# Three edits to a 12-stage decoder kernel: half-width value projections, array halves in turn, a bias on another engine, tables loaded last

## The reference

```python
# "table" attention: layer 0 self (rope) and cross (ctx), layer 2 router block (rank), layer 3 cross (mask)
q, k, v = xn @ Wq + bq, kv @ Wk + bk, kv @ Wv + bv          # kv = xn or the context rows
p = softmax(q @ k.T * scale + table)                        # table: a bias per head, 64 x 64
x = x + (p @ v) @ Wo + bo
# linear attention: layer 1 self
fq, fk = elu(q) + 1, elu(k) + 1
s = (fk @ fq.T) * (key index <= query index)
y = xn + ((s.T @ v) / (s.T @ 1 + 1e-6)) @ Wo + bo
# dense block that ends layer 2 self-attention
x = x + y + gelu(norm(y) @ W1 + b1) @ W2 + b2
```

## Time and profile before

| | |
|---|---|
| median of 3 runs | 7626.08 us (7619.54 to 7646.74) |
| profiled execution, its own time | 7625.12 us |
| its span, first to last instruction | 7623.3 us |
| PE busy over the span | 6668.1 us (87%) |
| DVE, ACT, POOL busy | 5380.2, 4152.7, 2881.5 us |
| mean granted TensorE clock | 0.950 |

### The profile page before, as it was taken

One profiled execution on the slowest core, in us unless ns is written; L12 is line 12 of the kernel. 1 busy time (PEld: TensorE's weight loads), 2 busy tenths in 40 slices (PEclk: granted clock), 3 DMA queues, 4 the chain that ended last, 5 costly groups with the idle time before them and its releaser, 6 DMA issues. The chain is left out here.

```text
span 7623.3 us, 190380 instructions
## 1 busy us (share of the span) xinstructions
PE 6668.1 (87%) x75040; PEld 4091.5 (54%) x75040; DVE 5380.2 (71%) x8861; ACT 4152.7 (54%) x6107; POOL 2881.5 (38%) x1663
## 2 busy tenths in 40 slices
PE   7989994887687989979988968989889999989898
PEld 5766683443442333333333345667566676667676
DVE  7877465575546999969999944668567777768444
ACT  3555333565435777767777754546444444446433
POOL 3311163332214888868787800146012121111000
PEclk9999996999888999989999989999999999999999
DMA  1000001000001222212222100000000000000000
GB/s 27 0 17 15 2 0 17 3 3 2 8 2 52 75 72 73 76 56 78 72 70 72 67 3 18 12 4 0 3 29 2 2 2 2 2 13 14 13 0 22
DMA packets 117004, 191.53 MB, mean 25 GB/s; under 512 B 39542, under 2 KB 75420, under 8 KB 116060
## 3 DMA queue, kind: packets, MB, share of 16 engines
q1 hardware_dynamic: 116572, 185.25, 7.7%
HBM read 174.99 MB, written 8.09 MB: 24 GB/s over the span
## 5 line engine op out<-in xcount | busy, mean ns | idle before, releaser
L2461 POOL TENSOR_TENSOR m_dBx<-m_dtx,m_Bs 128x1024 f32<-128x1024 f32 x518 | 1211.2, 2355 | 211.6 <-DVE m_hs L2798 169.3
L2798 DVE TENSOR_TENSOR_SCAN m_hs<-m_ps_dA,m_dBx 128x512 f32<-128x512 f32 x1036 | 1207.4, 1207 | 87.0 <-POOL m_dBx L2461 77.0
L2577 PE MATMUL m_ps_y<-m_yc,ident 128*128 128x512 f32 x2072 | 1050.9, 630 | 0.0
L2670 ACT ACTIVATE m_ps_dA<-m_dt,m_A 128x504 f32<-128x504 f32 x1036 | 687.0, 678 | 474.3 <-DVE m_hs L2798 471.6
L1998 POOL TENSOR_TENSOR a_s<-a_s,a_den 128x1024 f32<-128x1024 f32 x128 | 243.5, 1902 | 1144.9 <-DVE a_den L2044 1144.9
L2809 DVE TENSOR_TENSOR m_yc<-m_hs,m_ps_C 128x1024 f32<-128x1024 f32 x518 | 620.2, 1197 | 2.8 <-PE m_ps_C L2560 2.2
L2577 PEld LDWEIGHTS m_ps_y<-m_yc,ident 128*128 128x128 f32 x2072 | 358.0, 193 | 367.6 <-issue 367.6
L2560 PE MATMUL m_ps_C<-m_parts,m_sel 48*128 48x512 bf16 x520 | 204.2, 393 | 205.0 <-DVE m_yc L2809 204.9
L2560 PEld LDWEIGHTS m_ps_C<-m_parts,m_sel 48*128 48x128 bf16 x520 | 48.2, 93 | 609.4 <-DVE m_yc L2809 451.1
L580 POOL TENSOR_TENSOR c_kbd<-c_kf,c_hmask 128x1024 f32<-128x1024 f32 x66 | 125.0, 1894 | 524.8 <-ACT c_kf L493 514.1
L2042 DVE TENSOR_REDUCE a_den<-a_s 128x16 f32<-128x1024 f32 x128 | 156.0, 1219 | 206.0 <-ACT a_s L1950 206.0
(11 more groups left out here) (745 smaller groups left out, 16397.9 us busy)
## 6 DMA issues: line engine op xcount, KB each, us to landing
m_Bs<-m_BC_rows SPq DMA_DIRECT2D x260, 512.0 KB, 3.6
c_kvb<-in_ctxT SPq DMA_DIRECT2D x68, 128.0 KB, 2.0
c_kvb<-in_ctxT SPq DMA_DIRECT2D x17, 256.0 KB, 2.6
out_dram<-X SPq DMA_DIRECT2D x1, 4096.0 KB
m_BC_rows<-m_low SPq DMA_DIRECT2D x34, 64.0 KB, 2.9
m_part_rows<-m_split SPq DMA_DIRECT2D x34, 48.0 KB, 1.7
m_parts<-m_part_rows SPq DMA_DIRECT2D x34, 48.0 KB, 1.7
m_piece<-m_BC_rows SPq DMA_DIRECT2D x34, 32.0 KB, 1.7
```

Source lines behind the costliest of these rows:

```text
L2461: return nc.gpsimd.tensor_tensor(to, one, other, ALU.mult)
L2577: last = nc.tensor.matmul(ps_y[:, m, :], C.ident[:], of[:, m, :], start=s == 0, stop=s == NS - 1)
L2670: nc.scalar.activation(seqs(ps_dA[:, h % 3, :]), seqs(dt[:, par, m, :]), ACT.Exp, scale=A[:, m, s:s + 1]).then_inc(decay, 1)
L2798: nc.vector.tensor_tensor_scan(hs[:, s % HS, m, :], ps_dA[:, (2 * s + m) % 3, :], dBx[:, s % BX, m, :], 0.0, ALU.mult, ALU.add).then_inc(s ...
```

## The change

1. `values` in both attention functions multiplies with one half of `wv` per partition half (`wv_of(e)`: the 64 columns of the even or odd heads, in runs of eight), so each matmul streams 64 columns and not 128, and `ps_b` holds the 32 * 8 numbers of a sequence's half densely. `diagonal_values` reads them without gaps.
2. In `attn16_linear`, `weigh_values` takes the two partition halves in turn inside each head pair.
3. `attn16_table` loads the table, the mask, `wo` and `bo` last, on a semaphore of their own (`late_loaded`); PE waits for `loaded` and `prepared` after the first transposes, ACT after the first normalised rows; the table is prepared by a new function `prepare_table`, called on VectorE after the first values are taken, and PE waits for `table_ready` ahead of the first scores.
4. `gelu_ffn` drops L2922: `b2` is loaded to all 128 partitions and VectorE adds it to X. VectorE makes the normalised rows two groups ahead of the sum that it takes.

```diff
-        loads = [(wq, W["wq"]), (wo, W["wo"]), (wk, W["wk"]), (wv, W["wv"]), (hmask, W["hmask"])]
+        loads, late = [(wk, W["wk"]), (wq, W["wq"]), (wv, W["wv"]), (hmask, W["hmask"])], [(wo, W["wo"])]
         if rank:
             loads += [(tril, W["tril"]), (g1, W["g1"]), (wr, W["wr"])]
         else:
-            loads.append((table, W["table"]))
+            late.insert(0, (table, W["table"]))
         if cross:
-            loads += [(bo, bc(W["bo"], [P, D])), (bq, W["bq"]), (bk, W["bk"]), (bv, W["bv"])]
+            loads += [(bq, W["bq"]), (bk, W["bk"]), (bv, W["bv"])]
+            late.append((bo, bc(W["bo"], [P, D])))
...
         if mask:
-            loads.append((keepi, W["mask"]))
+            late.insert(0, (keepi, W["mask"]))
...
             if cross:
                 for par in range(2):
                     load(par, slice(par * UC, par * UC + UC))
+            for to, of in late:
+                sp.dma_start(to[:], of).then_inc(late_loaded, 16)
...
         @block.tensor
         def _(pe):
-            pe.wait_ge(loaded, n_loaded)
-            pe.wait_ge(prepared, n_prepared)
...
                 for s in range(USEQ):
                     for b in range(2):
-                        last = nc.tensor.matmul(ps_b[S * b:S * b + S, s * D:(s + 1) * D], kvb[:, par, s * S:(s + 1) * S], wv[:],
-                                                start=True, stop=True)
+                        last = nc.tensor.matmul(ps_b[S * b:S * b + S, s * HV:(s + 1) * HV], kvb[:, par, s * S:(s + 1) * S],
+                                                wv_of(b), start=True, stop=True)
...
             turn_rows(0)
+            pe.wait_ge(loaded, n_loaded)
+            pe.wait_ge(prepared, n_prepared)
             keys(0, 0, 0, True)
...
+            else:
+                pe.wait_ge(table_ready, 1)
+            pe.wait_ge(late_loaded, n_late)
             scores(0, 0)
...
+            act.wait_ge(scaled, 1)
             normalise_rows(0)
             rows_copy(0, 0)
             normalise_rows(1)
+            act.wait_ge(loaded, n_loaded)
+            act.wait_ge(prepared, n_prepared)
             key_copy(0, True)
...
+            def prepare_table():
+
+                dve.wait_ge(late_loaded, n_late)
+                if mask:
...
+                nc.vector.memset(mx[:], 0.0).then_inc(table_ready, 1)
+                dve.drain()
...
             take_keys(1)
             take_queries(1)
+            if not rank:
+                prepare_table()
...
             def weigh_values(w, par):
                 pe.wait_ge(masked, w + 1)
                 pe.wait_ge(vbd_ready, w + 1)
-                for s in range(USEQ):
-                    t, b = s // 2, s % 2
+                for t in range(UT):
                     for n in range(NB):
-                        last = nc.tensor.matmul(o_acc[S * b:S * b + S, t, 2 * n:2 * n + 2, :].rearrange("p h v -> p (h v)"),
...
+                        for b in range(2):
+                            s = 2 * t + b
+                            last = nc.tensor.matmul(o_acc[S * b:S * b + S, t, 2 * n:2 * n + 2, :].rearrange("p h v -> p (h v)"),
...
-        w1, w2, b1, b2 = sb("w1", [P, F]), sb("w2", [P, NF, D]), sb("b1", [P, NF]), sb("b2", [1, D])
+        w1, w2, b1, b2 = sb("w1", [P, F]), sb("w2", [P, NF, D]), sb("b1", [P, NF]), sb("b2", [P, D])
...
                     for c in range(NF):
-                        nc.tensor.matmul(o, hid[:, c, p * P:(p + 1) * P], w2[:, c, :], start=c == 0, stop=False)
-                    last = nc.tensor.matmul(o, C.ones[0:1, :], b2[0:1, :], start=False, stop=True)
+                        last = nc.tensor.matmul(o, hid[:, c, p * P:(p + 1) * P], w2[:, c, :], start=c == 0, stop=c == NF - 1)
...
             fr.dve(0)
+            dve.wait_ge(fr.xT_done, 1)
+            fr.dve(1)
+            dve.wait_ge(loaded, n_loaded)
             with dve.Fori(0, C.NG) as i:
-                dve.wait_ge(fr.xT_done, i + 1)
-                fr.dve(i + 1)
                 nc.vector.tensor_tensor(rows(C.X, i), rows(C.X, i), rows(C.Y, i), ALU.add)
+                dve.drain()
+                nc.vector.tensor_tensor(rows(C.X, i), rows(C.X, i), bc(b2[:].unsqueeze(1), [P, TPG, D]), ALU.add)
+                dve.wait_ge(fr.xT_done, i + 2)
+                fr.dve(i + 2)
                 dve.drain()
                 dve.wait_ge(out_done, i + 1)
```

More of the change, by code:

```diff
@@ L197 @@
 VW = HD + 1
+HV = NB * HD
 def attn16_table(C, name, mode, W, kT_dram=None):
@@ L245, in attn16_table @@
         seqs = lambda a: a.rearrange("p (s k) -> p s k", k=S)
-        loaded, prepared = sem("loaded"), sem("prepared")
+        wv_of = lambda e: wv[:].rearrange("p (n e d) -> p e n d", n=NB, e=2)[:, e, :, :]
+        loaded, prepared, late_loaded, table_ready = sem("loaded"), sem("prepared"), sem("late_loaded"), sem("table_ready")
         kv_loaded = [sem("kv_loaded0"), sem("kv_loaded1")]
@@ L271, in attn16_table @@
         if mask:
-            loads.append((keepi, W["mask"]))
-        n_loaded = 16 * len(loads)
+            late.insert(0, (keepi, W["mask"]))
+        n_loaded, n_late = 16 * len(loads), 16 * len(late)
         n_prepared = 2
@@ L659, in _ @@
                 ts(sinq[:], sinT[:], HD ** -0.5, None, ALU.mult)
[L660 to L669, removed]
             if cross:
@@ L676, in _ @@
                 nc.vector.tensor_copy(identb[:], C.ident[:])
-            else:
+            nc.vector.memset(mv[:], 0.0)
+            dve.drain()
+            nc.vector.memset(st[:], 0.0).then_inc(prepared, 1)
+            dve.drain()
+            def prepare_table():
+                dve.wait_ge(late_loaded, n_late)
+                if mask:
+                    nc.vector.tensor_copy(keep[:], keepi[:])
+                    dve.drain()
+                    ts(keep[:], keep[:], 0.0, None, ALU.not_equal)
+                    dve.drain()
+                    ts(off[:], keep[:], BIG, -BIG, ALU.mult, ALU.add)
+                    tt(table[:], table[:], bc(keep[:].unsqueeze(1), [P, NH, S]), ALU.mult)
+                    dve.drain()
+                    tt(table[:], table[:], bc(off[:].unsqueeze(1), [P, NH, S]), ALU.add)
                 for x in range(2):
@@ L884, in values @@
                     for e in range(2):
-                        last = nc.tensor.matmul(ps_b[S * e:S * e + S, s * D:(s + 1) * D], xnT[:, par, s * S:(s + 1) * S], wv[:],
-                                                start=True, stop=True)
+                        last = nc.tensor.matmul(ps_b[S * e:S * e + S, s * HV:(s + 1) * HV], xnT[:, par, s * S:(s + 1) * S],
+                                                wv_of(e), start=True, stop=True)
                 last.then_inc(v_done, 1)
@@ L1089, in diagonal_values @@
                     r = slice(S * e, S * e + S)
-                    own = ps_b[r, :].rearrange("p (s n e d) -> p s n e d", s=USEQ, n=NB, e=2)[:, :, :, e, :]
+                    own = ps_b[r, 0:USEQ * HV].rearrange("p (s n d) -> p s n d", s=USEQ, n=NB)
                     bias = bv[r, :].rearrange("p (n e d) -> p n e d", n=NB, e=2)[:, :, e, :]
@@ L2896, in gelu_ffn @@
         block = ctx.enter_context(nc.Block())
-        loads = [(w1[:], W["w1"]), (w2[:], W["w2"].rearrange("(c p) d -> p c d", p=P)), (b1[:], W["b1"]), (b2[:], W["b2"]),
+        loads = [(w1[:], W["w1"]), (w2[:], W["w2"].rearrange("(c p) d -> p c d", p=P)), (b1[:], W["b1"]), (b2[:], bc(W["b2"], [P, D])),
                  (g[:], W["g"]), (be[:], W["be"])]
```

17 lines of the change are left out of this document (8 added, 9 removed).

## The result

The changed kernel takes 7507.42 us (median of four runs, 7492.08 to 7525.66) against 7622.81 for the kernel before (four runs beside it): 115 us less by the medians. The ratio on record is 0.9841, 95% interval 0.9824 to 0.9859, which is 121 us less. The forecast was 135 less, 7491, with a range of 7462 to 7545. The profiled execution is the longest of the four, 7525.66 us with a span of 7523.9.

What follows compares the result with a forecast made beforehand. The prediction took PE's own order of work to bound the loops of the changed stages. Its terms, 56 + 41 + 30 + 8 = 135 us off 7625.1, gave 7490, forecast as a median of 7491, range 7462 to 7545.

Steps and rivals of the forecast that it cites:

- Linear attention in turn: Stage a1: alternating halves, with half values, brings a slot from about 8.3 to 6.48 us, 56 us over 31 slots.
- The rival that alternating gains nothing: Stage a1: slow slots stay, 0.32 us saved a slot, 10 us for 56, total 7537; chance 0.05.
- Half values: Four table stages: each `values` call 0.32 us shorter in 32 slots a stage, 41 us together.
- Is PE the bound in all four table stages?: Step checking DVE's waits for PE in f2 (0.58 us a slot) and a0 (1.3); concluded 0.32 fits under both.
- My list of what the profile would show: Expected signs after the change, among them table slots 0.3 us shorter and L332 at 0.5 us.
- the rival at 7537: Values don't get shorter because the gapped operand halves the pace; 41 us goes, a1 takes 5 more; chance 0.14.
- the one on the other side: Slower than before: the gapped operand in `values` is read far slower, number by number; 7806 at three times today's call; chance 0.02.
- Dense stage: Stage m3: second product starts at 4.48 and takes 4.33, group 8.81 us for 10.68, 30 us over 16 groups.
- The bound of 36 us: Stage m3: upper bound of the gain, if L2921 could follow the transposes at 4.08 us after the group's start.
- Tables last: Table stages' starts: scores start earlier; c3 gains 3.8, c0 3.3, a0 1, f2 0, together 8 us.
- the 1.3 us given back: Starts of c3 and c0: first scores run at the lower clock after PE's idle time, costing 1.3 us.
- Clock rivals: a1's clock still falls every second slot, 23 us, 7514, chance 0.12; table stages' clock falls, 95 us, 7586, chance 0.03.

Runs made afterwards that it cites:

- e1_turn_only: Kernel before, with only linear attention weighing the partition halves in turn, values at full width: 7584.86 us, ratio 0.9938.
- e10_moved: Kernel after with split waits of `e5_split`, table values between second and third transposes, linear attention's queries and keys ahead of `weigh_values`: 7468.73 us, ratio 0.979.
- e5_split: Kernel after, with the table stages' `weigh_values` waiting for each of ACT's four copies ahead of the quarter reading it: 7466.34 us, ratio 0.9785.
- e6_before_split: Kernel before, with `weigh_values`' wait for ACT's copies split in four, values at full width: 7646.72 us, one run.
- e8_contig: Kernel after, with VectorE copying the table stages' `wv` once into two halves without gaps: 7520.32 us, one run.
- e4_late_only: Kernel before, with only the table stages' late loads and table preparation last, values at full width: 7612.11 us, ratio 0.9977.
- e12_bias_dve: Kernel after, with VectorE still adding the dense stage's bias but making rows one group ahead as before: 7533.51 us, one run.

## Why the prediction was right, and where its terms were off

- **The sum**, 135 us, against 121 by the ratio and 115 by the medians. It came out this near by luck in part: two errors of opposite sign met, 27 too much in the values and 10 too little in the dense stage. That the page's sixth and seventh slices were low for a1's sake was a misreading; the argument stood on the windows and slots, which were right.
- **Linear attention in turn**: right in its steps. `weigh_values` takes 1.98 us to the next call (2.03 taken), slots 5.98 and 7.03 (6.48 forecast as their mean), PE waits for `qbd`, the clock is full in the loop, and the stage gives 56.4 us (56). Of these, 35 are the 1.13 us by which 31 slots are shorter than 7.62, and 20 are the slow slots: 13 of 31 in the kernel before, at 9.10 to 9.18 us (the mean was 8.25, and 8.3 was taken). The stage's mean clock is 0.93 and not 0.97, since its first 32 us run at 0.52, which the forecast hadn't counted. `e1_turn_only` showed the same for W = 6.43 (6.70 for 6.64). The rival that alternating gains nothing fell, and with it the rule that I had weighed: the page "TensorE: Matmul & The Clock Gate", section "Part 3: Packing small matmuls", of the Trainium skill lets a weight load overlap only with other row groups in use; here both halves use all 128 rows, and the time went from 50 to 30 ns a record. What in this order keeps the clock up isn't shown: the run of short matmuls is shorter, and PE pauses 0.46 us a slot now. In `e10_moved` c0's loop is at 1.00 with PE at work 259.35 of 260 us, so work without pauses is not enough to lower it.
- **Half values**: the term that was off, 41 us forecast and 14 to 16 arrived. The price of the call was right, even low (0.36 less and not 0.32). The step that failed is "Is PE the bound in all four table stages?". It looked for DVE's slack only. The call stands between the last transposes of probabilities and `weigh_values`, which waits for all four of ACT's copies of them, and it had covered the last of those copies with 0.11 us to spare. Of the 0.36 us that the call lost, 0.30 went into that wait (0.76 between the two calls' starts and not 0.46); the rest, with 0.05 of `weigh_values`, is the 0.11 that a slot gained. `e5_split` gave it back, `e6_before_split` showed that it wasn't there before. My list of what the profile would show named the slots 0.3 shorter; that is where it was wrong.
- **Gaps in the operand**: the rival at 7537, and the one on the other side, had the operand cost time. `e8_contig` shows it cost none (222 ns a record in the median with gaps and without).
- **Dense stage**: start of the second product right at 4.48; its length mis-sized, 4.33 forecast and 3.57 measured. I took off the bias matmuls' own 4 * 0.42 and kept 0.135 us for each of the others; freed of their neighbours they take 0.112. 0.76 * 16 = 12 us, of which 10 show in the stage. The bound of 36 us was too low for the same reason. That DVE's additional sum costs nothing held: its waits for PE are 2.73 us a group.
- **Tables last**: 8 forecast, 8.1 measured in `e4_late_only`, c3 3.6 (3.8), c0 1.3 (3.3). The mis-sized term is the 1.3 us given back. In c0 of `e4_late_only` the first scores start 4.1 us earlier than before (4.6 forecast), but their two calls take 2.74 and 1.82 us for 1.47 and 1.12, and the next slot's second call 2.01 for 1.12: about 3 us back. In c3 it is about 3 as well, but there the scores start 6.2 us earlier in that kernel and 7.2 in the whole change, for 5.1, since the loads landed 4.8 us into the stage and not 6.4. That the sum is met all the same is luck.
- **Clock rivals** for a1 and the table stages didn't happen: c0 is at 0.96 as before, and full in its loop.

## What to carry to other kernels

Ahead of making an instruction shorter, look at what the instruction behind it waits for, and when that arrives: an engine with a busy share of 90% can still be covering another engine's last copy. A wait for several parts of which only the last is late should stand ahead of the part that needs it. Where an edit shortens a loop, look also for the next loop through another engine; moving one piece of PE's order to relieve POOL lengthened the way through DVE.

## What the runs showed that was not expected

- Two column halves that alternate take 30 ns a record with 128-row weights, and 50 in a row on one half.
- A matmul with one row of weights between others with 128 costs more than its own rows: 0.42 us each when it stands behind every eight, 0.27 when the four stand together, and the others go from 0.136 to 0.112 us a record.
- The granted clock fell in five of fourteen groups of the dense stage with the bias matmuls first (0.85 against 1.00, 1.6 us each), though PE had work 8.95 of 9.73 us in the groups ahead; with 7.7 us of work in 8.51 (`e12_bias_dve`) it never fell. What sets it off there stays open.
